# Attention with a loop body of eight pairs of heads instead of four

## What is computed

```python
mod = (silu(c) @ wmod).reshape(4, 6, 1, -1)            # sa, ca, ga, sb, cb, gb
h = layernorm(x) * (1 + ca) + sa
q = (h @ wq + bq)   # 32 heads of 32;  k, v: 8 heads of 32, each shared by 4 query heads
att = softmax(q k^T / sqrt(32));  a = att v
x = x + ga * (a @ wo + bo)
h = layernorm(x) * (1 + cb) + sb
x = x + gb * lora_moe(h)                               # 4 experts of rank 16, the top 2 of them
```

## Time and profile before

| | |
|---|---|
| median of 3 runs | 3176.2 us (3172.26 to 3180.29) |
| the profiled execution's own time | 3167.2 us |
| its span, first to last instruction | 3165.4 us |
| `attend`, by PE's clock and idle time | about 665 to 2611 us of the span |
| its loop, by the branch instructions | 812.5 to 2490.5 us |
| PE, DVE, ACT, POOL busy, share of the span | 95%, 62%, 49%, 57% |

### The profile page before, as it was taken

The page is one execution under the profiler, slowest core; times in us unless marked ns, Lnnn a source line. Parts: engine busy times, 40 slices in busy tenths (PEclk is TensorE's granted clock), DMA queues, the critical chain, the costliest instruction groups (busy, mean ns, idle before and its releaser), DMA issues. The chain is left out here.

```text
span 3165.4 us, 49778 instructions
## 1 busy us (share of the span) xinstructions
PE 3014.9 (95%) x15590; PEld 1742.8 (55%) x15590; DVE 1960.9 (62%) x2572; ACT 1566.5 (49%) x2906; POOL 1796.5 (57%) x595
## 2 busy tenths in 40 slices
PE   5899999979999999999999999999999987999997
PEld 3788888844444444444444444444444435777776
DVE  4433343257767777777677677677777735666665
ACT  2111111126666666666666666666666662444444
POOL 2333333247777778778778778777787784211110
PEclk9899999979999999999999999999999998999999
DMA  6433434241122121121221221221211104333331
GB/s 228 163 135 130 147 118 154 98 132 46 35 53 48 35 52 43 40 53 36 46 52 34 49 52 34 49 50 37 49 43 43 39 11 157 100 100 99 97 96 67
DMA packets 156453, 241.46 MB, mean 76 GB/s; under 512 B 48992, under 2 KB 90400, under 8 KB 156320
## 3 DMA queue, kind: packets, MB, share of 16 engines
q1 hardware_dynamic: 156320, 240.05, 26.2%
HBM read 159.12 MB, written 79.82 MB: 75 GB/s over the span
## 5 line engine op out<-in xcount | busy, mean ns | idle before, releaser
L853 DVE TENSOR_REDUCE mx<-s_ps 128x1 f32<-128x1024 f32 x1024 | 1234.0, 1224 | 530.6 <-PE s_ps L926 527.8
L833 ACT ACTIVATE p_t<-st_ps 128x512 f32<-128x512 f32 x2048 | 1174.4, 598 | 708.5 <-PE st_ps L951 586.7
L791 POOL TENSOR_TENSOR p_sum<-p_sum,p_t 128x2048 f32<-128x2048 f32 x256 | 1171.6, 4577 | 22.1
L951 PE MATMUL st_ps<-q_st,k_st 98*128 98x512 f32 x2048 | 918.8, 454 | 24.2 <-ACT p_t L833 17.8
L951 PEld LDWEIGHTS st_ps<-q_st,k_st 98*128 98x128 f32 x2048 | 382.2, 187 | 753.7 <-ACT p_t L833 529.3
L926 PE MATMUL s_ps<-k_st,q_st 96*128 96x512 f32 x2048 | 658.7, 403 | 14.8 <-DMA q_st<-q_hi_d 11.1
L965 PE MATMUL num_ps<-p_t,v_sb 128*32 128x512 f32 x4096 | 545.5, 605 | 0.9 <-ACT p_t L833 0.9
L791 POOL TENSOR_TENSOR p_sum<-p_t 128x2048 f32<-128x2048 f32 x64 | 293.2, 4581 | 429.2 <-ACT p_t L833 429.2
L926 PEld LDWEIGHTS s_ps<-k_st,q_st 96*128 96x128 f32 x2048 | 389.1, 192 | 74.0 <-DVE mx L853 15.5
L372 POOL TENSOR_TENSOR o_lo<-side,o_hi 128x512 fp32r<-128x512 f32 x80 | 104.7, 1309 | 340.7 <-ACT o_hi L342 340.7
L1220 POOL TENSOR_TENSOR a_lo<-a_f,a_hi 128x1024 fp32r<-128x1024 f32 x32 | 76.2, 2382 | 389.0 <-ACT a_hi L1255 388.9
(11 more groups left out here) (129 smaller groups left out, 2812.8 us busy)
## 6 DMA issues: line engine op xcount, KB each, us to landing
q_st<-q_hi_d SPq DMA_DIRECT2D x128, 256.0 KB, 4.4
stage<-w_mod SPq DMA_DIRECT2D x48, 512.0 KB, 5.5
q_hi_d<-o_hi SPq DMA_DIRECT2D x64, 256.0 KB, 2.0
q_lo_d<-o_lo SPq DMA_DIRECT2D x64, 256.0 KB, 2.0
q_st<-q_lo_d SPq DMA_DIRECT2D x64, 256.0 KB, 4.2
att_d<-a_sb SPq DMA_DIRECT2D x128, 128.0 KB, 2.3
a_f<-att_d SPq DMA_DIRECT2D x32, 512.0 KB, 4.7
x_sb<-x SPq DMA_DIRECT2D x32, 512.0 KB, 5.4
```

Source lines behind the costliest of these rows:

```text
L791: nc.gpsimd.tensor_tensor(total, before, p_t[:, kt, :, :], ALU.add).then_inc(sum_done, 1)
L833: nc.scalar.activation(p_t[:, s, c, :], st_ps[:, c % 2, :], ACT.Exp, scale=SCALE)\
L853: nc.vector.tensor_reduce(mx[:, slot % 2, e:e + 1], s_ps[:, e % 2, :], AX_X, ALU.max)\
L951: nc.tensor.matmul(st_ps[:, c % 2, :], k_st[:, slot // 2, s * P:(s + 1) * P], q_st[:, slot, jj, h * QW:(h + 1) * QW], start=True, stop=True)\
```

## The change

The loop body of `attend` holds eight calls of `do` instead of four, on every engine. The loop now has 7 rounds instead of 14, over the same pairs 4 to 59. The slot stays the pair's number modulo 4, and the combination's number the pair's number over 2, so that every engine issues the same work on the same buffers in the same order. The first four and the last four pairs stay straight code.

```diff
+    BODY = 2 * QR
...
-            with eng.Fori(1, NPAIR // QR - 1) as n:
-                for slot in range(QR):
-                    do(n * QR + slot, slot, n * 2 + slot // 2)
+            with eng.Fori(0, (NPAIR - 2 * QR) // BODY) as n:
+                for at in range(BODY):
+                    do(n * BODY + (QR + at), at % QR, n * (BODY // 2) + (QR + at) // 2)
```

More of the change, by code:

```diff
@@ L613, in attend @@
     FIRST = 18
-    assert KT == NKT and NS == 16 and RAWS == 2
+    assert KT == NKT and NS == 16 and RAWS == 2 and (NPAIR - 2 * QR) % BODY == 0 and BODY % QR == 0
     START_PLAN = [(1, e) for e in range(FIRST - NS, NS)] + [(2, e) for e in range(NS // 2)]
```

## The result

The changed kernel takes 3188.39 us (median of 11 runs, 3182.35 to 3195.45), the kernel before in the same comparison 3172.34 (3169.50 to 3181.17): 16.05 us more, a ratio of 1.0048 with a 95% interval of 1.0036 to 1.0060. That is slower by more than the 0.3% of the forecast's "same", and inside its range of 3168 to 3200. The profiled execution has a span of 3187.2 us.

What follows compares the result with a forecast made beforehand. PE's stream was taken to bound the kernel (busy 95% of the span); PE's fetches 15.6 plus clock falls 4.2 less ACT's branches 11.7 gave +8.1 us, forecast 3184 us, range 3168 to 3200.

Steps and rivals of the forecast that it cites:

- same: Forecast outcome that the time stays within about 0.3% (9.5 us) of the kernel before; chance 0.49.
- The branch of before: Attention loop before: each branch back costs about 0.9 us through ACT's code fetch, 11.7 us for 13.
- PE fetches: PE's doubled body of some 2890 instructions is fetched at each branch back: 2.6 us late, 15.6 for six.
- The clock: TensorE's clock falls behind PE's pause at three of six branches, 1.4 us each: 4.2 us.
- The other engines: DVE, POOL and SP bodies double too; DVE's may become too long, but its wait adds nothing.
- Streaming: PE fetching code in the middle of the attention loop's body costs nothing.
- The sum: Whole kernel: 15.6 + 4.2 - 11.7 = +8.1 us, giving 3184 us.
- the second rival: Clock falls at nearly every attention-loop branch: +12.3 to +19.5 us, 3189 to 3196; chance 0.33 together with PE waiting twice.
- the double wait: One fetch is not enough behind a branch, so PE waits twice; same slower side, sharing the 0.33.
- the likeliest one: PE fetches and the clock falls at none to about half of the branches: 3184 us; chance 0.50.
- The first rival: PE's code stays at hand, ACT alone pauses 6 times instead of 13: -6.3 us, 3170; chance 0.17.
- the third: Rival: a branch's cost is not fetching but something per round whatever the length; gives the first rival's time.

Runs made afterwards that it cites:

- the short body of ACT: ACT's loop body holds two pairs, all other engines four, against the kernel before: 3162.68 us against 3174.62, ratio 0.9949.
- the straight version: All 56 pairs of the attention loop in one body on every engine, against the kernel before: 3154.34 us; with 180 instructions ahead of PE's first loop 3147.71.

## Why the prediction was right, and where not

*The branch of before.* Right. The price was 11.7 us for 13 branches and is 12.0; it belongs to ACT's fetch, which two kernels show by taking it away in different ways.

*PE fetches.* Right, and shown by giving PE's length and the others' length to different kernels. The pause was put at 2.6 us from ACT's 3.0 and the packets' size, and is 15.8 / 6 = 2.64; 15.6 us were forecast for six. It varies more than a single number says, 2.24 to 3.12. The Trainium skill (Runtime: NRT & Kernel Launch, section Instruction fetch mechanics) gives PE room for 2048 instructions and the others for 512, and the runs agree as far as they go: PE keeps a body in seven pieces of 256 with the next one ahead and loses it in eight, ACT keeps three pieces of 128 and loses four. What I held open with it, how 342 could be too many for 512, is solved by counting pieces: the body lies in four of them and the next one is fetched as a fifth. Two things on that page differ from the traces. ACT's pieces are of 8 KB here, where it gives 16; and it counts a target as at hand only in a window of two pages of 256 instructions, while PE's body of before, about 1450, branches back in 0.2 us. The prediction put the whole room in place of that window.

I read q14 as ACT's queue; it carries DVE's code too (result section). The packets of before are ACT's all the same, so nothing in the sum hangs on it.

*The clock.* This is the term that was mis-sized. "I let it fall at three of six branches", at 1.4 us each, 4.2 us in sum. It fell at five, and two of the falls were long ones of 2.5 and 2.8: 9.5 us. The prices, 1.4 for a short fall and 2.6 for a long one from rows in other stages, hold to within 0.2 us. The number of falls failed: a pause of 2.33 us that left the clock alone was taken as a sign that 2.6 might do so every other time, but in the loop PE paused 2.26 us and the clock fell, and 2.24 us and it didn't. With PE's body moved (eight pairs, 100 instructions ahead) it fell behind 2.35 us and not behind 2.71, so the length of the pause alone does not decide. One row on each side does not make a threshold: over the four kernels in which PE waits in this loop, the clock fell behind 16 of 19 pauses of 2.2 to 3.2 us.

*The other engines.* Right. DVE's body did become too long, and waits 2.8 to 3.3 us with packets of its own. In the changed kernel the six long pairs are explained by PE's pause and the clock; with PE's code kept, DVE's wait adds at most 0.25 us a branch to ACT's (pairs of 30.76 to 30.87 us against 30.62).

*Streaming.* Right: other pairs take 29.71 us in both kernels.

*The sum.* +8.1 us was forecast and +13.3 is what the stage shows, the difference being the clock. The medians differ by 16.05; whether the rest is scatter in the first stage's loop was not separated. In the traces of the eight kernels with that stage unchanged, the first copy of `attend` stands between 729.0 and 744.3 us, earliest in that of before. That the time came out within 4.4 us of the 3184 is luck in part: the forecast was added to a median of three runs, 3176.2, which lay 3.9 us above that of eleven, 3172.34, and the step itself is 16.05 us where 8.1 was forecast. So the case that came true is the second rival, the clock falling at nearly every branch (+12.3 to +19.5, 3189 to 3196), at 0.33 together with the double wait, and not the likeliest one. The first rival, PE's code at hand, and the third, a cost whatever the length, are refuted by the 13 packets a round and by the short body of ACT.

## What to carry to other kernels

The length of a loop body has a good range for each engine apart: look at which "instruction" queue moves packets round after round, and at the time from an engine's branch to its next instruction. Make short the body of the engine that waits there, or leave the loop away, and do not lengthen all of them together; on the engine that bounds the kernel a pause of 2 to 3 us cost its clock as well in 16 of 19 cases here. A few dozen instructions more ahead of a loop can decide whether it is kept, so a small unrelated edit may move the time by some 0.3%, and such a step should be looked for before an edit is credited with it.

## What was not expected of the hardware

- **Where code lies decides.** 45 idle instructions ahead of ACT's loop saved about 12 us in the stage's trace, and with 180 ahead of PE's first loop the attention stage starts 8.6 us earlier in the trace of the straight version (first copy at 728.4 us instead of 737.0). In the medians that is 6.6 us (3154.34 to 3147.71), measured in two comparisons whose kernels before differ by 2.5.
- **A branch at a piece's border is kept or lost by chance.** PE's body in the first stage ends where a piece of 256 instructions ends. In some executions the fetch of the next piece starts close to the branch (up to 0.2 us ahead of it in 11 of 12 cases, 0.5 behind in one), which then takes 3.9 to 4.5 us; in others no packet comes there, and it takes 0.2. Part of the scatter of up to 17 us among runs of one kernel may be this: with the 180 instructions ahead, the six runs of either kernel lie within 4.6 us. Only the profiled executions show the branches themselves.
- **The clock fell after short pauses too.** With PE's body of four pairs and the others' of eight, PE paused 1.06 us, and a little later the clock was at its low level; the pair after that took 31.37 us. With PE's body of eight and the others' of four it did so behind one of ACT's seven pauses, of 0.86 us. In the kernel before it did so behind none of 13 pauses of 0.9 us. The pause and the stretch, first of 1.06 us, then of 0.86:

```profile
1063.20 0.50 PE L952 MATMUL st_ps<-q_st,k_st 98*128 98x512 f32 x1 [1.06 <-ACT p_t L834]
```
```profile
1065.70:1068.90 3.20, 3.20 (x17) 0.60 (x16) 0.91 (x1) 0.70 (x2) 0.00 (x0) 0.50 0.25 64
```
```profile
1670.86 0.50 PE L952 MATMUL st_ps<-q_st,k_st 98*128 98x512 f32 x1 [0.86 <-ACT p_t L834]
```
```profile
1673.50:1676.40 2.90, 2.90 (x17) 0.60 (x16) 0.76 (x1) 0.60 (x1) 0.00 (x0) 0.50 0.30 69
```
